# End of the turns of a fused attention and FFN kernel: an earlier release of two projections, and the clamp of the eight-bit chunks split between ScalarE and VectorE

## The reference

```python
def _quantize_elem(x, ebits, mfrac, max_norm):
    priv = jnp.maximum(jnp.floor(jnp.log2(jnp.where(x == 0, 1.0, jnp.abs(x)))), float(-2 ** (ebits - 1) + 2))
    scale = jnp.exp2(priv - mfrac)
    return jnp.clip(jnp.round(x / scale) * scale, -max_norm, max_norm)

def _quantize_mx(x, ebits, mfrac, emax_elem, max_norm):      # blocks of 32 along the last axis
    amax = jnp.max(jnp.abs(xb), axis=-1, keepdims=True)
    scale = jnp.exp2(jnp.clip(jnp.floor(jnp.log2(amax)) - emax_elem, -127.0, 127.0))
    return _quantize_elem(xb / scale, ebits, mfrac, max_norm) * scale

_q_act = lambda x: _quantize_mx(x, 2, 3.0, 2.0, 7.5)
_q_w = lambda w: _quantize_mx(w, 2, 1.0, 2.0, 6.0)
_mx_linear = lambda x, w: jnp.einsum('bsh,oh->bso', _q_act(x), _q_w(w))

x = x + attn(cond(x, fside, cond_512, w1, u1))               # wkv, then attention, one batch at a time
y = cond2(x, fside, cond_512, w2, u2)
gate, up = _mx_linear(y, w_gate), _mx_linear(y, w_up)
x = x + _mx_linear(jax.nn.silu(gate) * up, w_down)
```

## Time and profile before

| | us |
|---|---|
| median of three runs | 903.3 |
| lowest and highest | 902.97 and 903.76 |
| profiled execution, its own time | 902.48 |
| its span | 900.7 |

### The profile page before, as it was taken

The page is one execution under the profiler, slowest core; times in us unless marked ns, Lnnn a source line. Parts: engine busy times, 40 slices in busy tenths (PEclk is TensorE's granted clock), DMA queues, the critical chain, the costliest instruction groups (busy, mean ns, idle before and its releaser), DMA issues.

```text
span 900.7 us, 10845 instructions
## 1 busy us (share of the span) xinstructions
PE 757.4 (84%) x3985; PEld 388.7 (43%) x3985; DVE 772.7 (86%) x1122; ACT 468.3 (52%) x710; POOL 73.8 (8%) x149
## 2 busy tenths in 40 slices
PE   4667649298789999988899999887999999989696
PEld 1222224145444444455444444554444444654584
DVE  4999999998999879989998799899987897443787
ACT  4965645348566362485763623856645325353340
POOL 1000000111100002111000021110000121100000
PEclk9786778699999999999999999999999999999797
DMA  9623310445400003754000028640000185400001
GB/s 335 247 84 105 105 58 17 88 110 157 109 13 24 1 12 94 199 152 118 13 24 1 12 64 219 162 107 22 24 2 12 29 206 131 102 1 1 1 1 47
DMA packets 30820, 72.27 MB, mean 80 GB/s; under 512 B 5808, under 2 KB 6832, under 8 KB 28976
## 3 DMA queue, kind: packets, MB, share of 16 engines
q1 hardware_dynamic: 19584, 46.67, 17.4%
q0 software_dynamic: 6144, 16.79, 7.9%
q10 hardware_dynamic: 5040, 8.14, 2.8%
HBM read 33.82 MB, written 4.19 MB: 42 GB/s over the span
## 4 chain that ended last, share of the span: by engine, by line
PE 51%; DVE 30%; issue 7%; ACT 6%; DMA 3%; POOL 1%; SPq 1%; ACTq 0%; DVEq 0%
PE bank L1524 9%; PE bank L1331 7%; PE bank L1419 6%; PE bank L1408 5%; PE bank L1536 5%; PE bank L1323 4%; DVE negmax L1056 4%; PE bank L1390 3%; PE bank L1435 3%; DMA stacks<-rows 2%; PE bank L1357 2%; ACT region L546 2%; DVE num L950 2%; PE bank L1392 2%; DVE fn L936 1%
## 5 line engine op out<-in xcount | busy, mean ns | idle before, releaser
L318 POOL DMA_DIRECT2D stacks<-rows x128 | 69.8, 553 | 707.5 <-DVE region L833 346.6
L546 ACT ACTIVATE region<-bank 128x384 f32<-128x384 f32 (+1 forms) x192 | 95.8, 523 | 59.1 <-PE bank L1393 56.5
L1056 DVE TENSOR_REDUCE negmax<-bank 128x4 f32<-128x512 f32 (+2 forms) x96 | 98.6, 1035 | 30.1 <-PE bank L1360 17.3
L1390 PE MATMUL bank<-stacks 128*128 128x512 f32 (+3 forms) x256 | 105.3, 417 | 20.4 <-ACT region L546 20.0
L1331 PE MATMUL bank<-h,wqkv 128*128 128x512 f32 x256 | 115.1, 601 | 4.2 <-DVE region L1284 4.2
L1357 PE MATMUL bank<-stacks 128*128 128x128 f32 (+3 forms) x256 | 77.2, 395 | 13.4 <-DVE negmax L1056 7.8
L1392 PE MATMUL bank<-maxrow,pick 128*128 128x512 bf16 (+3 forms) x256 | 81.4, 318 | 0.0
L1331 PEld LDWEIGHTS bank<-h,wqkv 128*128 128x128 f32 x256 | 48.4, 193 | 61.4 <-issue 55.4
L1390 PEld LDWEIGHTS bank<-stacks 128*128 128x128 f32 x256 | 50.1, 196 | 50.0 <-ACT region L546 40.3
L1323 PE MATMUL bank<-wqkv,h 128*128 128x512 f32 x128 | 60.9, 620 | 4.7 <-DVE h L984 4.7
L1577 PE MATMUL bank<-region,ident 128*128 128x512 f32 x64 | 48.8, 921 | 12.4 <-DVE identb L887 12.4
(11 more groups left out here) (178 smaller groups left out, 1484.1 us busy)
## 6 DMA issues: line engine op xcount, KB each, us to landing
stacks<-rows SPq DMA_DIRECT2D x128, 128.0 KB, 4.0
stacks<-rows POOLq DMA_DIRECT2D x128, 128.0 KB, 4.7
kt<-in_fside ACTq DMA_DIRECT2D x30, 256.0 KB, 3.3
region<-in_w_gate SPq DMA_DIRECT2D x4, 1024.0 KB, 11.0
h<-in_x SPq DMA_DIRECT2D x4, 1024.0 KB, 5.7
xt<-in_x SPq DMA_DIRECT2D x4, 1024.0 KB, 7.5
region<-in_w_up SPq DMA_DIRECT2D x4, 1024.0 KB, 5.6
region<-in_w_down SPq DMA_DIRECT2D x4, 1024.0 KB, 4.7
```

The source lines that it names most:

```text
L318: eng.dma_start(stacks[HD * r:HD * r + HD, at:at + 2, i, :].bitcast(F32), rows[mine, q:k + 1:k - q, :]).then_inc(stacked[s][i], 16)
L546: nc.scalar.activation(probs[:, i, P_AT[tiles[0]]:P_AT[tiles[0]] + columns], bank[4 + n % 2][:, 0:columns], ACT.Exp, scale=SCALE).then_inc ...
L1056: nc.vector.tensor_reduce(o, scored, AX_X, ALU.max, negate=True).then_inc(max_taken, 1)
L1390: nc.tensor.matmul(o, ks[s][:, i, P * t:P * t + P], qs[s][:, i, P * t:T], start=True, stop=False, skip_group_check=True)
```

## The change

In the first three turns, the first two of the three projections wait for `silu_ready` alone, and only the third for `inter_ready`. The clamp is no longer read from the eight-bit chunk: ScalarE copies the chunk to bf16 first (`widen`), and VectorE clamps that copy in place. Chunks alternate between two eight-bit buffers (`q8` and the second quarter of `ratio2`) and two bf16 ones (`q16` and `xq`). VectorE rounds chunk n (`round_8`) before it clamps and scales chunk n - 1 (`clamp_and_scale`).

```diff
+        eighths = [q8, ratio2[:, 1, :].bitcast(FP8).rearrange("p (j t) -> p j t", j=4)]
+        wide = [q16, xq]
...
+            def widen(b, n):
+
+                act.wait_ge(rounded_8, b * FC + n + 1)
+                if n >= 2:
+                    act.wait_ge(iq_ready, b * FC + n - 1)
+                nc.scalar.activation(wide[n % 2], eighths[n % 2], ACT.Copy).then_inc(widened, 1)
...
+                    for n in range(FC):
+                        widen(b, n)
                     copy_raw(b + 1, 3)
...
+            def round_8(b, n):
+
+                if n == 0:
+                    carry()
+                nc.vector.tensor_tensor(eighths[n % 2], inter[:, 4 * ROUNDING[n]:4 * ROUNDING[n] + 4, :], over(inv[:, :]),
+                                        ALU.mult, saturate=False).then_inc(rounded_8, 1)
+
+            def clamp_and_scale(qc, b, n):
+
+                dve.wait_ge(widened, b * FC + n + 1)
+                qc.link(nc.vector.tensor_scalar(wide[n % 2], wide[n % 2], E2M3_MAX / 64, -E2M3_MAX / 64, ALU.min, ALU.max))
+                nc.vector.tensor_tensor(inter_q[ROUNDING[n]], wide[n % 2], over(scale_b[:, :]), ALU.mult).then_inc(iq_ready, 1)
...
-                for c in ROUNDING:
-                    round_acts(qc, inter[:, 4 * c:4 * c + 4, :], inter_q[c]).then_inc(iq_ready, 1)
+                round_8(b, 0)
+                for n in range(1, FC):
+                    round_8(b, n)
+                    clamp_and_scale(qc, b, n - 1)
+                clamp_and_scale(qc, b, FC - 1)
...
+                pe.wait_ge(silu_ready, (b + 1) * (FJ // 2))
+                for s in range(2):
+                    project_qk(b + 1, 1, s)
                 pe.wait_ge(inter_ready, (b + 1) * (FJ // 2))
-                if more:
-                    for s in range(2):
-                        project_qk(b + 1, 1, s)
-                    project_qk(b + 1, 3, 0)
+                project_qk(b + 1, 3, 0)
```

More of the change, by code:

```diff
@@ L228, in adaln_attention_ffn @@
         iq_ready = sem("iq_ready")
+        rounded_8 = sem("rounded_8")
+        widened = sem("widened")
         down_ready = sem("down_ready")
@@ L1629 @@
 SLOT_BEHIND = ({1: 0, 2: 1, 4: 2, 7: 3, 9: 4, 11: 5}, {2: 2, 5: 3, 8: 4, 11: 5})
-QUANT_STEPS = 35
+QUANT_STEPS = 31
 STACK_INC = 4 * 16
```

## The result

The changed kernel takes 909.68 us (median of four runs, 908.32 to 910.52) against 903.53 for the kernel before on the same footing: a ratio of 1.0068, 95% interval 1.0055 to 1.0081. Two later timings of the same kernel gave 1.0048 and 1.0087; why they differ is part of what follows.

A forecast was written before the change was run, and what follows sets the result against it. Neither PE nor DVE alone was taken as the bound; the end of PE's down projection sets the next turn. A later start (1.35) plus a clock fall (1.5), 2.85 us a turn, 8.55 in three, gave 911.8 us, range 907.0 to 914.0.

The forecast's parts named there:

- What bounds the place: Ends of the first three turns: PE's down projection sets the next turn; first chunk without slack of note, last 0.3 us.
- The earlier release: Projections start right behind the up sums, 1.55 us sooner; the gain is worth only as much as the first chunk is earlier.
- The rounding: On DVE and ACT: first chunk ready 1.8 us later, at 346.95, the rounding as a whole ending 2 us sooner.
- the hand-overs: Between DVE's instructions up to the first chunk: 0.1 us added to the summed durations.
- the additions' wait: On DVE, additions wait for PE's down sums for about 5 us instead of 0.53, and start near 366.
- The clock: Behind PE's 2.8 us idle time the clock falls in all three turns, 1.5 us each; 910.0 to 912.5, chance 0.70.
- the clock stays, or falls in one or two turns: Rival for the clock behind PE's idle time ahead of the first down matmul: 907.4 to 910, chance 0.18.
- The sum: Over three turns: 1.35 + 1.5 = 2.85 us a turn, 8.55 in all, with nothing given back in the next turn.
- What was held to be covered: ACT's raw copy, the stacks' DMAs and the high parts at the turn's end cost nothing, all covered by about 1 us.

The follow-up runs named there:

- the release alone: The kernel before with only the earlier release of two projections (waiting for silu_ready), the rounding as before: 904.04 us, ratio 1.0000.
- giving back the first chunk alone: The changed kernel with chunk 0 clamped straight from eight bits and scaled ahead of everything else, the other three through ScalarE: 904.51 us, ratio 1.0002.
- the rounding alone: The changed kernel with PE's waits as in the kernel before, so only the rounding is changed: 908.04 us, ratio 1.0042; timed again 905.89 us, 1.0034.
- stacks early: The changed kernel with SP and POOL issuing group 0's stacks of the next batch at the second rounded_8 instead of iq_ready: 910.15 us, ratio 1.0069.
- two experiments that ended the down projection sooner: The changed kernel with chunk 0 clamped from eight bits as before (904.51 us, 1.0002), or with the last projection ahead of the first chunk (903.25 us, 0.9989).
- both filled kernels: The changed kernel with three unused matmuls (2.6 us) in front of the third projection, timed twice: 910.59 us, ratio 1.0079, and 909.24 us, 1.0067.

## Why the prediction was right, and where its sizes were off

**What bounds the place.** Right: both ends of the rounding stand close to PE, and the first chunk decides in the changed kernel. Only the slack of the first chunk was misread: the release alone shows 0.5 us, not a tenth. The sum didn't suffer, as it counted from the matmul at 345.71 and not from the chunk. The release alone was worth nothing (1.0000, bound by the last chunk), the later first chunk alone cost what the changed kernel lost at a clock of 1.00, and giving back the first chunk alone took the loss away (1.0002).

**The earlier release.** Right to the hundredth: relative to the start of the rounding the projections begin 1.55 us sooner.

**The rounding.** Right in order and kinds. The clamp took 0.69 us, the bound that was taken, and the copy from eight bits 1.91 where 1.875 was assumed. That row reads a bank; the copy from int16 that reads the same memory as this one took 1.91 us (mean 1910 ns) in the kernel before already:

```profile
L729 ACT ACTIVATE region<-region 128x2048 bf16<-128x2048 int16 x4 | 7.6, 1910 | 20.6 <-DVE region L866 20.6
```

The first chunk came 1.54 us later, and 1.8 was forecast. The term was mis-sized in the hand-overs: durations were added with 0.1 us on top, while behind both multiplications the next DVE instruction starts 0.09 and 0.07 us before their rows end (341.76, 343.96 and 346.17 are 2.20 and 2.21 apart, not 2.29). So the first chunk takes 6.35 us and not 6.60. So PE stood still for 2.54 to 2.56 us and not 2.8, and was 1.07 us later and not 1.35, which makes 0.8 us over three turns. The last chunk was ready 2.5 us sooner; it helped nothing, as the additions' wait of 4.07 us instead of 0.53 shows (5 were forecast).

**The clock.** The step that failed. Falls behind the idle time were put at all three turns, with a chance of 0.70; they came in one of three, and in 4 of 12 such idle times of 2.54 to 2.56 us over four profiles. In the two profiles of the rounding alone, where the idle time is in two pieces of 1.39 and 0.9, there is none in six; that speaks for a part of the release in the falls, but is too little to show it. The price of one was right (1.5 forecast, 1.55 to 1.69 measured). The step took it that behind a longer idle time a fall is surer, because no idle time of 1.75 us or more in the one profile of before went without. The other profiles don't bear that out: with the release alone the clock stayed at 1.00 behind 2.04 and 3.05 us in the last turn, while falls are seen behind 1.40 in several. A matmul of the release alone, and the clock there:

```profile
888.26 1.92 PE L1445 MATMUL bank<-h,down_q 128*128 128x256 bf16 x16 [3.05 <-DVE h L833]
```

```profile
888.00:889.00 1.00, 0.74 (x7) 1.00 0.00 0
889.00:890.00 1.00, 1.00 (x11) 1.00 0.21 77
```

The warning of the Trainium skill ("TensorE: Matmul & The Clock Gate", section "Why this matters for your kernels") of longer gaps than this agrees with the eight that went without one, and not with the four that didn't. The case that came true was the second one, "the clock stays, or falls in one or two turns", 907.4 to 910, which had a chance of 0.18.

**The sum.** Forecast 3 x 2.85 = 8.55; by its own terms the profile has 3 x 1.07 + 1.69 = 4.9 at the three places. That the profiled execution is nevertheless 8.1 longer is due to 1.41 us ahead of the first rounding and 1.78 in an attention part that the change doesn't touch, most of this by a longer wait for stacks. Nothing in the sum stands for these 3.2 us; they filled the place of the falls that didn't come. So the mechanism of the first chunk was right by reasoning, and that 911.8 came within 2.1 us was luck.

**What was held to be covered.** The raw copy, the stacks and the high parts were covered, as said (stacks early: no gain). That cover was thin, 0.6 us (the high parts end at 364.79, PE takes them up at 365.43): two experiments that ended the down projection sooner met it at once.

**Open.** Why the clock falls in some turns and not in others with the same instructions; whether the ends of the turns are all that the release costs, since the changed kernel has 1.0068, 1.0048 and 1.0087, and the rounding alone 1.0042 and 1.0034; what sets the wait for the stacks inside the turns, 1.47 to 3.16 us; and why the stacks landed late in the middle turn of both filled kernels.

## What to carry to other kernels

When a consumer takes chunks one after the other at about the rate at which they are made, look at the first chunk: software pipelining over two buffers shortens the chain as a whole, but puts one more stage ahead of the first result, and here the first result came 1.54 us later, of which 0.47 was slack and 1.07 a turn was lost, while 2.5 us at the other end gained nothing. Before making a producer faster, find work for the consumer that doesn't need it, and check who else waits for the same semaphore; moving one projection and one DMA wait turned a loss of 0.7% into a gain of 0.35%. And idle time of TensorE ahead of a dense stretch has a price beyond its length, which comes in some turns and not in others, so one profile isn't enough to size it.

## What the runs showed of the hardware

- ScalarE copies 128x2048 from eight bits to bf16 in 1.91 us, as from int16 in the same memory (1.91); out of a bank int16 takes 1.875.
- VectorE clamps 128x2048 in bf16 in place in 0.69 us; the same clamp from eight bits takes 1.22.
- Behind VectorE's instructions of 1.2 and 2.3 us the next one starts 0.07 to 0.09 us before their rows end where it has nothing to wait for (0.03 us after the end behind the clamp of 0.69), so a chain is to be added up from starts.
- After 2.54 to 2.56 us of idle time of PE the clock went to 0.50 in 4 of 12 cases, and each fall made the stretch 1.55 to 1.69 us longer. In other places falls came behind 1.40 us, and once none behind 3.05 (the release alone, last turn).
- The stretches without a fall agree over kernels with the same rounding and order to 0.01 us, so apart from the falls what spreads the times of these kernels isn't there. The wait for the DMAs of stacks in the third turn spreads from 1.47 to 3.16 us.
